# Convolutions as 64x32 products, from a ring of shifted copies in SBUF

## What is computed

```
x = x + L0(gn(x))    # rfft2, a complex 3x3 convolution, + bias, irfft2
x = x + L1(gn(x))    # every channel row block times a gate of 0 or 1
x = x + conv2d(gn(x), W)                  # layer 2: 3x3, 16 -> 16 channels, padding 1
x = x + conv2d(gn(x), weight)             # layer 3: 3x3, 16 -> 16 channels, padding 1

def _gn(v, G=8, eps=1e-5):
    B_, C_, H_, W_ = v.shape
    g = v.reshape(B_, G, C_ // G, H_, W_)
    m = jnp.mean(g, axis=(2, 3, 4), keepdims=True)
    s = jnp.var(g, axis=(2, 3, 4), keepdims=True)
    return ((g - m) / jnp.sqrt(s + eps)).reshape(v.shape)
```

## Time and profile before

| | |
|---|---|
| Timed, median of 3 runs | 4808.68 us (4795.11, 4808.68, 4819.33) |
| Profiled execution, span | 4801.7 us |
| TensorE busy in it | 4548.2 us, 95% |
| VectorE, ScalarE busy | 2925.9 us (61%), 2487.6 us (52%) |
| First layer of the second image, 716 to 1040 us | 324 us |
| First convolution, mean of 8 | 108.2 us |
| From its end to the second convolution, second image | 10.1 us |
| Second convolution, mean of 8 | 117.6 us |
| DMA | 468.11 MB, mean 97 GB/s |

### The profile page before, as it was taken

How to read it: one execution, slowest core, us unless ns; L and a number is a source line. 1 busy time by engine, 2 the same in 40 slices (tenths; PEclk the granted TensorE clock), 3 DMA queues, 4 the chain that set the end, 5 groups by cost and what they waited for, 6 DMA issues and landing times.

```text
span 4801.7 us, 221653 instructions
## 1 busy us (share of the span) xinstructions
PE 4548.2 (95%) x84784; PEld 2936.4 (61%) x84784; DVE 2925.9 (61%) x10604; ACT 2487.6 (52%) x7085; POOL 3.2 (0%) x14
## 2 busy tenths in 40 slices
PE   4999999999999999999999999999999999998889
PEld 1555675556655566556665556655666557655566
DVE  1777717766277662777527765377744777257770
ACT  4455355544555445554455544555445554544435
POOL 0000000000000000000000000000000000000000
PEclk8999999999999899999999989999899999999999
DMA  7443015630166202662036510366004650034304
GB/s 196 111 124 100 4 29 172 176 102 4 47 177 176 79 3 61 178 177 63 4 86 177 176 41 3 105 176 174 24 3 120 177 163 19 3 111 122 90 4 143
DMA packets 290069, 468.11 MB, mean 97 GB/s; under 512 B 25392, under 2 KB 92144, under 8 KB 289264
## 3 DMA queue, kind: packets, MB, share of 16 engines
q1 hardware_dynamic: 289392, 458.29, 33.1%
HBM read 323.98 MB, written 134.22 MB: 95 GB/s over the span
## 4 chain that ended last, share of the span: by engine, by line
PE 91%; DVE 3%; issue 3%; DMA 1%; SPq 1%; ACT 1%; ACTq 0%; DVEq 0%
PE ps L1247 35%; PE ps L1165 19%; PE ps L1150 18%; PE ps L1158 6%; PE ps L1174 5%; PE ps L1024 5%; DMA x<-x 1%; PE ps L1273 1%; PE ps L1070 1%; PE ps L1071 0%; PE ps L1097 0%; PE ps L1305 0%; PE ps L1219 0%; SPq L360 0%; PE ps L1112 0%
## 5 line engine op out<-in xcount | busy, mean ns | idle before, releaser
L1247 PE MATMUL ps<-x,conv_s 32*32 32x512 f32 x49104 | 1728.0, 603 | 20.8 <-DVE x L948 16.7
L1247 PEld LDWEIGHTS ps<-x,conv_s 32*32 32x32 f32 x49104 | 1252.8, 103 | 437.9 <-issue 196.1
L563 ACT ACTIVATE x<-ps,vec 128x256 f32 (+1 forms) x1024 | 492.0, 495 | 1003.1 <-PE ps L1165 1003.1
L1165 PE MATMUL ps<-hil,shared 128*128 128x256 f32 x4096 | 993.6, 386 | 0.0
L814 DVE COPY vsb<-ps 128x512 f32<-128x512 f32 x512 | 329.9, 686 | 1043.6 <-PE ps L1150 1043.6
L1165 PEld LDWEIGHTS ps<-hil,shared 128*128 128x128 f32 x4096 | 740.2, 190 | 273.8 <-issue 194.1
L802 DVE SCALAR_TENSOR_TENSOR shared<-xin,trig 128x256 f32<-128x256 f32 x2048 | 821.6, 441 | 57.3
L629 ACT ACTIVATE x<-ps,vec 64x512 f32<-64x512 f32 (+1 forms) x768 | 527.2, 686 | 395.9 <-PE ps L1247 385.6
L1150 PE MATMUL ps<-shared 32*32 32x512 f32 x16384 | 656.4, 605 | 0.0
L620 ACT ACTIVATE x<-ps,vec 128x512 f32 x512 | 347.9, 685 | 439.6 <-PE ps L1247 439.6
L1150 PEld LDWEIGHTS ps<-shared 32*32 32x32 f32 x16384 | 306.2, 104 | 280.0 <-issue 216.8
(11 more groups left out here) (170 smaller groups left out, 2720.6 us busy)
## 6 DMA issues: line engine op xcount, KB each, us to landing
xin<-x SPq DMA_DIRECT2D x512, 256.0 KB
out<-x SPq DMA_DIRECT2D x512, 256.0 KB
shared<-x SPq DMA_DIRECT2D x448, 256.0 KB, 5.0
shared<-t_strip SPq DMA_DIRECT2D x512, 96.0 KB, 3.6
x<-x SPq DMA_DIRECT2D x64, 256.0 KB, 8.1
x<-t_proj SPq DMA_DIRECT2D x1, 2048.0 KB, 11.8
hil<-t_hil SPq DMA_DIRECT2D x1, 560.0 KB, 12.1
trig<-t_trig SPq DMA_DIRECT2D x1, 512.0 KB, 11.8
```

The lines of the kernel that those rows point to most:

```text
L563: ins = nc.scalar.activation(split_in(strip_of(s))[:, q, :], split_in(ps[:, bank, :])[:, q, :], ACT.Identity, bias=v1(MEAN), accum_out=sum ...
L1165: mm = pe.matmul(split_in(ps[:, BY + 2 * odd + e, :])[:, int(q < 2), :], xt[:, e, q, :], hil[:, q, 0:HALF], start=False, stop=True, skip_g ...
L1247: mm = pe.matmul(ps[TM * cg:TM * cg + TM, banks[k], :], conv_s[TM * rg:TM * rg + TM, kw, second, :], x1[TM * rg:TM * rg + TM, of, kw:kw + ...
```

## The change

**Products.** Each product contracts over 64 partitions, so one product replaces the two halves: an output block takes 3 products of 64 x 32 weights, a pair 24, on the eight 64x32 tiles. taps, halved and the lags are gone; products issues, per tap, the four blocks of both strips in turn. The weights are laid out anew by CONV_BLOCKS.

**Copies.** Four input rows starting at an even row are four neighbouring rows of a strip for every second output block only. For the others the rows are copied, shifted by two rows (32 partitions), into a ring of RING = 4 pairs of strips. SyncE issues them as SBUF-to-SBUF DMAs: seven a pair in the first convolution (six of 32 partitions, one of 64; copy2) and four in the second (two of 96, two of 32; copy3), each partition 2 KB. A pair's copies wait for its gates and for the end of the pair four earlier; TensorE waits for copied before each pair.

**Squares.** ScalarE squares the even strips in evict2, after both evictions of a pair; VectorE the odd ones, straight into cols.

**Room.** The ring lies over planes. So VectorE's make_planes of the next image waits until all but two pairs of the second convolution are done, and for the second pair of strips until all are. The ring's pad columns are set once by GpSimd and once by VectorE. The correction of the bias takes 12 products instead of 24. In the last image the stores run four pairs behind the copies, and the last eight follow at the end.

```diff
+RING = 4
+COPIES2, COPIES3 = 7, 4
+CONV_BLOCKS = ((0, 0, 0), (1, 0, 1), (2, 0, 0), (3, 0, 1), (1, 1, 0), (3, 1, 1))
...
+            def copy_blocks(n, odd, to, s, of):
+
+                sp.dma_start(ring[to, 2 * (n % RING) + odd, 1:1 + N], x1[of, s, 1:1 + N]).then_inc(copied[n % RING], 16)
+
+            def copy2(i, n):
+
+                even = 2 * (PAIRS - 1 - n)
+                sp.wait_ge(gated, i * STRIPS + min(STRIPS, 2 * n + 3))
+                sp.sem_inc(s_sp, 1)
+                if n >= RING:
+                    sp.wait_ge(convolved, cv(i, 1 + n - RING + 1))
+                    sp.sem_inc(s_sp, 1)
+                copy_blocks(n, 1, slice(HP, HP + TM), even + 1, slice(P - TM, P))
+                copy_blocks(n, 1, slice(HP + TM, P), even + 1, slice(0, TM))
...
+                copy_blocks(n, 0, slice(0, HP), even, slice(TM, HP + TM))
...
+            def copy3(i, n):
+
+                if n < RING:
+                    sp.wait_ge(convolved, cv(i, 1 + PAIRS - RING + n + 1))
+                    sp.sem_inc(s_sp, 1)
+                    sp.wait_ge(evicted, ev(i, 1 + STRIPS))
+                    sp.sem_inc(s_sp, 1)
+                else:
+                    sp.wait_ge(convolved, cv(i, 1 + PAIRS + n - RING + 1))
+                    sp.sem_inc(s_sp, 1)
...
+                for odd in range(2):
+                    copy_blocks(n, odd, slice(0, P - TM), 2 * n + odd, slice(TM, P))
+                    copy_blocks(n, odd, slice(P - TM, P), 2 * n + odd + 1, slice(0, TM))
...
                 for n in range(PAIRS):
+                    copy2(i, n)
+                for n in range(PAIRS):
+                    copy3(i, n)
                     if more and n >= PAIRS - (STRIPS - DEFERRED):
-                        sp.wait_ge(evicted, ev(i, 1 + STRIPS + 2 * n + 2))
-                        sp.sem_inc(s_sp, 1)
                         store(i, n - (PAIRS - (STRIPS - DEFERRED)))
-                    elif not more:
+                    elif not more and n >= RING:
                         for e in range(2):
-                            store(i, 2 * n + e)
+                            store(i, 2 * (n - RING) + e)
...
+                    act.wait_ge(evicted, ev(i, 1 + 2 * n + 1))
+                    act.wait_ge(a_c_squared, i * PAIRS + n + FREE)
+                    nc.scalar.activation(junk2, strip_of(STRIPS - 2 - n * 2), ACT.Square,
+                                         accum_out=cols[:, 3, bass.ds(STRIPS - 2 - n * 2, 1)]).then_inc(a_c_squared, 1)
...
+                dve.wait_ge(convolved, cv(i, -2))
+                dve.sem_inc(s_dve, 1)
                 for k in range(2):
                     make_planes(steps_of(k), k, k, u0 + 1, 0)
+                dve.wait_ge(convolved, cv(i, 0))
+                dve.sem_inc(s_dve, 1)
...
+                def products(banks, slot, outputs, strips, kw):
+
+                    for j in range(TILES):
+                        for k in range(2):
+                            cg, h, from_ring, kind = outputs(strips[k])[j]
+                            rows = slice(HP * h, HP * h + HP)
+                            of = ring[rows, slot + k, kw:kw + N] if from_ring else x1[rows, strips[k], kw:kw + N]
+                            mm = pe.matmul(ps[TM * cg:TM * cg + TM, banks[k], :], conv_s[rows, kw, kind, :], of,
+                                           start=(kw == 0), stop=(kw == TAPS - 1), skip_group_check=True)
+                    return mm
```

More of the change, by code:

```diff
@@ L32 @@
 PAIRS = STRIPS // 2
-DEPTH2, LAG2 = 4, TAPS + 1
-DEPTH3, LAG3 = 3, TAPS
+DEPTH2, DEPTH3 = 4, 3
+RING = 4
+COPIES2, COPIES3 = 7, 4
+COPIED = PAIRS // RING * (COPIES2 + COPIES3)
+CONV_FREE = 3
 CONVOLVED = 1 + 2 * PAIRS
@@ L112, in tables @@
     eye_conv = np.zeros((P, 2, TAPS, 2, TM))
-    for rg in range(TILES):
+    for rg, kind, second in CONV_BLOCKS:
         for c in range(C):
-            eye_conv[TM * rg + C + c, :, 1, 0, c] = 1.0
-            eye_conv[TM * rg + c, :, 1, 1, C + c] = 1.0
+            if second:
+                eye_conv[TM * rg + c, :, 1, kind, C + c] = 1.0
+            else:
+                eye_conv[TM * rg + C + c, :, 1, kind, c] = 1.0
     zsel = np.zeros((ZR, P + ZR))
@@ L162, in placed @@
         for kw in range(TAPS):
-            for second in range(2):
+            for rg, kind, second in CONV_BLOCKS:
                 for r in range(2):
@@ L167, in placed @@
                         if 0 <= kh < 3:
-                            for rg in range(TILES):
-                                for c in range(C):
-                                    convs[TM * rg + C * r + c, l, kw, second, C * o:C * o + C] = wt[:, c, kh, kw]
+                            for c in range(C):
+                                convs[TM * rg + C * r + c, l, kw, kind, C * o:C * o + C] = wt[:, c, kh, kw]
     return {"w_mix": mix, "w_u": uw, "w_bias": bias, "w_conv": convs}
@@ L251, in part @@
             return shared[:, taken - size:taken].rearrange(pattern, **dims)
+        junk = part("p (q w) -> p (q w)", q=2, w=HALF)
+        ring_at = taken
+        part("p (a w) -> p a w", a=1, w=2 * UNROLL)
         planes = part("p (k a w) -> p a k w", k=UNROLL, a=2, w=N)
+        wst = part("p (k v a m) -> p k v a m", k=UNROLL, v=2, a=3, m=TM)
+        ring = shared[:, ring_at:ring_at + 2 * RING * WIDE].rearrange("p (k w) -> p k w", w=WIDE)
+        wst_at = lambda k: UNROLL - 1 - k
         xa = part("p (k w) -> p k w", k=UNROLL, w=N)
@@ L445, in image @@
                 for n in range(PAIRS):
+                    copy2(i, n)
+                for n in range(PAIRS):
+                    copy3(i, n)
                     if more and n >= PAIRS - (STRIPS - DEFERRED):
-                        sp.wait_ge(evicted, ev(i, 1 + STRIPS + 2 * n + 2))
-                        sp.sem_inc(s_sp, 1)
                         store(i, n - (PAIRS - (STRIPS - DEFERRED)))
-                    elif not more:
+                    elif not more and n >= RING:
                         for e in range(2):
-                            store(i, 2 * n + e)
+                            store(i, 2 * (n - RING) + e)
+                if not more:
+                    for s in range(STRIPS - 2 * RING, STRIPS):
+                        store(i, s)
             image(0, True, False)
@@ L470, in _ @@
                 nc.gpsimd.memset(x1[:, :, 0:WIDE:WIDE - 1], 0.0).then_inc(pads_zeroed, 1)
+                nc.gpsimd.memset(ring[:, :, 0:WIDE:WIDE - 1], 0.0).then_inc(pads_zeroed, 1)
         @block.scalar
@@ L1303, in convolutions @@
                     for kw in range(TAPS):
-                        for f in range(2):
-                            mm = pe.matmul(stat[TM * t:TM * (t + 1), 4:5], conv_s[:, kw, f, :], vec[:, ZV:ZV + 1],
-                                           start=(kw == 0 and f == 0), stop=(kw == TAPS - 1 and f == 1))
+                        mm = pe.matmul(stat[TM * t:TM * (t + 1), 4:5], conv_s[:, kw, 0, :], vec[:, ZV:ZV + 1],
+                                       start=(kw == 0), stop=(kw == TAPS - 1))
                 mm.then_inc(p_bias3, 1)
```

137 lines of the change are left out of this document (61 added, 76 removed).

## The result

The kernel after takes **5230.97 us** (median of four runs, 5225.73 to 5235.87) against 4806.6 of before: 1.088 times as long, interval 1.086 to 1.090. The forecast was 4750, its range ended at 4900. The profiled execution's span is 5234.1 us, 432.4 over that of before.

The account below looks back on a forecast made before the run. TensorE, mainly the convolution products, was taken as the bound. Per image 7.0 - 16.6 - 1.1 + 0.6 = -10.1 us, -71 for seven, +10 for the last: -61, giving 4748, said as 4750 us; range 4570 to 4900.

Parts of the forecast that it names:

- TensorE's pair after: Both convolutions: a pair of strips on eight 64x32 tiles takes TensorE 2.6 us instead of 3.12, bounds 2.57 and 3.12.
- The tiles that gain nothing: Rival, both convolutions: TensorE's pair stays 3.12 us, so the second convolution keeps its 16.6 in seven images; 4866, chance 0.10.
- SyncE's price of an issue: Copies into the ring: each issue holds SyncE 0.422 us plus 0.04, with ends at 0.326 and 0.617.
- issues are dear: Rival, first convolution's 1792 issues: gain gone from 0.456 us an issue; 4925 at 0.52, about 5110 at 0.617; chance 0.21.
- The first convolution: SyncE becomes the bound at 3.45 us a pair; 115.2 us against 108.2, +7.0 us an image.
- The second convolution: TensorE stays the bound, SyncE needing 2.06 us a pair; 32 x (3.12 - 2.6) = -16.6 us an image.
- the term for the last eight pairs: Second convolution: an added store makes 2.9 us a pair, 0.3 over TensorE; the ring's three-pair lead takes up the 2.4.
- Bias correction: Just ahead of the second convolution: 24 records instead of 48, where 2.16 us stood; -1.1 us an image.
- Into the next image: Handover between images: VectorE can prepare the first two strips only when two pairs are left; +0.6 us an image.
- The last image: Copies and stores together need 3.8 us a pair; 122 us from second convolution to end against 117.7; +10 in all.
- Squares on ScalarE, VectorE: First convolution: ScalarE's three operations a pair take 2.07 us, VectorE loses half its squares; both cost nothing above 2.1 a pair.
- The clock: Rival, first convolution: the clock falls in TensorE's 0.85 us pauses, 435 us more, about 5180; chance 0.02.

Follow-up runs that it names:

- The first experiment: The kernel after with bursts of DMAs of several forms behind its last store, from SyncE, ScalarE and GpSimd; SyncE's issues took 0.59 us from SBUF, 0.42 from DRAM.
- merged: The kernel after with the second convolution's four copies a pair issued as two DMAs of both strips; alone 5169 us.

## Why the prediction was wrong

**The bound now; TensorE's pair after: right.** 2.58 us measured, 2.6 taken. The 0.55 us of a pair that are not streaming went with half the instructions, which are also on half as many tiles; no run has one without the other. The tiles that gain nothing (chance 0.10) are excluded by the run without copies. That the look-ahead of 64 instructions in the Trainium skill ("TensorE: Matmul & The Clock Gate", architectural detail) is the reason isn't shown by any run; the 2.57 that came out by it is what was measured.

**SyncE's price of an issue: the step that failed.** "The nearest are loads with plain rows on both sides." I ordered the rows by strides and by their number, took 0.422 with ends at 0.326 and 0.617, and missed that all plain ones came out of DRAM, while the ones out of SBUF, the stores, had a median of 0.674 and a minimum of 0.603. I put that down to strides. The first experiment has 0.421 against 0.590 for the same 32 rows. The price's share: 4.56 against 3.45 us a pair, 35.5 us an image, 284 in all; the run with copies from DRAM gives back 30.6 an image. My rival "issues are dear" was this case, with 0.617 at 5110. The estimate that I drew from the Trainium skill ("DMA: Bandwidth & Descriptors", why a DMA increments its semaphore by 16), 0.427 for any DMA, is close for DRAM sources (0.421, 0.432) and wrong for SBUF ones: 0.59.

**The first convolution.** Its form was right: SyncE without a pause, TensorE waiting for the ring. From SyncE's first copy (1100.73) to the end at 1263.61 it was 162.9 us where I had 110.4 + 2.3 + 3.2 = 115.9. The price is 35.5 of these 47.0, the twelve issues stalled by fetches 9.7, and I hadn't thought of those; 1.8 are left. The wait ahead of it was foreseen: 3.45 us of issue and 2.3 of landing, and TensorE starts 6.0 us after the first copy.

**The second convolution: half of the gain, -8.6 instead of -16.6.** I had 2.06 us of SyncE a pair; at 0.591 it is 4 x 0.634 + 0.21 = 2.75, over TensorE's 2.6. But in the first 24 pairs that costs nothing: TensorE's small products give SyncE the time. What failed here is the term for the last eight pairs, 2.9 us of SyncE each with a store, whose 2.4 us the ring's lead was to take up. They came 4.1 us apart, and TensorE waits 6.8 to 8.2 us there. Where GpSimd issues the copies and SyncE the stores alone, evictions are 2.58 us apart in these pairs too, and the stage takes 101.6 us on average, near the 102 that I had forecast. With copies from DRAM it is 103.3, merged 104.6.

**Bias correction: right**, -1.1 foreseen, -1.4 measured. **Into the next image:** +0.6 foreseen, 0.1 measured on average at the last mixing products, within a spread of 1 us either way.

**The last image: mis-sized.** 3.8 us a pair and 122 in all, by 276 GB/s of loads. Measured 190. With the same rows out of DRAM it is 147.0, so 43 of the 68 us between 122 and 190 go with the copies' source; with a quarter of their bytes and all the issues it is 167.7, with fewer issues on SyncE's queue 163 to 176. So issues and bytes both count. My rate came from loads alone, and the long issues of this stage, 47 us, weren't in the sum; what makes them stays open.

**Squares on ScalarE, VectorE:** free, as forecast; at 2.58 us a pair, too.

**The clock** did fall, as that rival had it: a granted clock of 0.94 in the first convolution shown and 0.87 in the last two, 1.00 without copies. But SyncE's queue, which had no pause, set the pace, so that the rival's 5180 lies near the measured 5231 is chance.

**Range and chances.** The break-even of 0.456 us follows from the sum, and I said that the margin was narrow; the chance of being above it, 0.21, rested on the wrong rows. The end of the range should have gone to the 0.617 that I had named as a bound. My 5110 for it is 4748 + 0.195 x 1792 = 5097 by my own sum, and leaves out that the second convolution would then need 4 x 0.657 + 0.21 = 2.84 us a pair of SyncE. By the span the forecast was 493 us short: 284 are the price in the first convolutions, 78 the fetches there, 14 the rest of them and the way in, 56 the second convolutions, 68 the last image; the two small terms give 6 back.

## What to carry to other kernels

When a change brings many small DMAs, count issues before bytes, and take the price from a row with the same kind of source; if there is none, the bounds are not a formality. Price the stretch where two kinds of traffic share a queue by itself: here the copies of the second convolution cost nothing until the stores stood behind them. Spread issues over queues that are idle (with four of seven on GpSimd, and the second convolution's merged, 8.8% slower became 3.5% faster) before making each DMA larger, since a larger one lands later and frees its slots later. And look at what else runs on the DMA engines: code written out costs its fetches.

## What the runs showed of the hardware

- A DMA issue with plain rows holds SyncE 0.58 to 0.60 us if its source is in SBUF (32 or 96 rows, 512 or 2048 bytes) and 0.42 to 0.43 if it is in DRAM (32 or 128 rows); ScalarE 0.61 and 0.44, GpSimd 0.498 for either at 32 rows.
- A fetch of 16 KB of TensorE's instructions lengthened the issue in progress on SyncE by 0.4 to 1.4 us; one comes for every 64 float32 products written out, and a loop of 32 products brought in one piece only in 640.
- Copies inside SBUF together with stores to DRAM moved 173 to 202 GB/s, copies from DRAM with the same stores 222, and stores alone, four in flight, 201; loads alone had 276, and copies of 96 rows inside SBUF alone 275 (5267 to 5271 us in the first experiment).
- 24 float32 products on eight 64x32 tiles took 2.58 us for the work that 48 on sixteen 32x32 tiles did in 3.12.
